# Banded attention per key tile on float32r halves, and split first loads of the full attention, in a two-layer kernel

## The chip, the cores and the metric

One core of one Trainium2 chip. The metric is the device time of one execution of the whole program in microseconds (us), lower is better. Clocks of the profile start at the first instruction of the profiled execution.

## What is computed

Two layers over x of shape (2, 2048, 256), 16 heads of 16 features. Layer 0 is full attention gated by an expert FFN, layer 1 is banded attention gated by a LoRA mixture:

```python
xn = _layernorm(x); s = _L0_attn_ref(xn, ...); g = _silu(_L0_ffn_ref(xn, ...)); x = x + s * g
xn = _layernorm(x); s = _L1_attn_ref(xn, ...); g = _silu(_L1_ffn_ref(xn, ...)); x = x + s * g

# inside _L1_attn_ref: a key counts for a query if it is at most 64 positions away
band = jnp.abs(idx[:, None] - idx[None, :]) <= WINDOW // 2          # WINDOW = 128
scores = jnp.einsum('bhqd,bhkd->bhqk', q, k) * SCALE + jnp.where(band, 0.0, -jnp.inf)
attn = jax.nn.softmax(scores, axis=-1)
out = jnp.einsum('bhqk,bhkd->bhqd', attn, v)
```

## The kernel before

The program is a chain of stages with a barrier of all engines between them: `phase_weights`, `phase_project` (layer 0), `phase_router`, `phase_attend_full`, `phase_combine_experts`, `phase_project` (layer 1), `phase_attend_band`, `phase_combine_lora`. In a stage each engine runs a program of its own, written out by hand, and semaphores tie them. SP issues the loads and stores, and a DMA is issued when the engine's program comes to it, in that order.

Projection (`phase_project`). Eight chunks of 512 tokens. TensorE makes q and k (four blocks of 128 features, `m`) and v; each block of q and k is split into summands that together hold the fp32 value. In layer 0 these are two float32r halves: ScalarE writes the first (L625), VectorE the rest (L543), and SP stores both to `s_halves`. In layer 1 they are three bf16 parts: ScalarE the first (L625), VectorE the remainder `rest` (L548), ScalarE the second part (L630), POOL the third (L472), and SP stores 128 x 3 x 512 bf16 per block to `s_parts` (L420). Per chunk SP also stores xT (four of 128 x 512 fp32, L401) and v (four, L427) and loads x.

Full attention (`phase_attend_full`). Eight groups of four heads, four iterations of 512 queries each. Two heads stand at rows 0 and two at row 64 (`side`), with three sets of 16 rows (high x high, high x low, low x high) and, for the scores, two rows more in which K is 1 and Q holds the two halves of minus the maximum. Before the scores of an iteration can be made, all its maxima must be known: TensorE makes score tiles for maxima (L1074), VectorE reduces them (L965, 32 units an iteration), TensorE turns the maxima, VectorE splits them, and POOL stores them into the rows of Q (`store_maxima`, L923). TensorE then makes the scores (L1100), ScalarE the exponentials (L1027), TensorE the product with V (L1112). At the start SP issues 30 loads of K and Q for group 0 (`load_halves`: per set of rows one of K, 16 x 2 x 2048, and four of Q, 16 x 2 x 512), then four of V; TensorE waits for all 30 and for the rows of ones. TensorE's program writes out iterations 0 to 7 and 24 to 31 and runs 8 to 23 in a loop of two rounds.

Banded attention (`phase_attend_band`). Again eight groups of four heads, in 32 chunks of 512 queries. K and Q hold six sets of 16 bf16 rows (`PART_ROWS`), a padding row with its two sides filled with -1e30, and two rows for the maximum, 99 in all; K is padded by 128 columns at both ends. For each of the 16 query tiles of a chunk TensorE makes a tile for maxima (97 x 128 by 256 keys, L1403), VectorE adds the mask and reduces (L1324), two chunks ahead of the scores. The maxima of a chunk are turned, split, and stored by POOL (`store_maxima`, L1275, two DMAs). Scores are made per chunk and key tile (`TILES`, six a chunk with widths 64, 192, 256, 256, 192, 64, so that tiles at a chunk's edge are made for both chunks), L1434, with the mask added by a product of the identity with the mask in bf16 (L1439). ScalarE takes the exponentials of four heads at once (L1367), TensorE multiplies with V (L1454). Outputs are turned (L1420), divided by VectorE (L1340) and stored by POOL (L1280). K and Q have two buffers; V has one, reloaded by quarters:

```python
with sp.Fori(1, NG - 1) as g:
    values(g)                      # waits for pv_done of the group before, quarter by quarter
    wait_apart(sp, kq_loaded, GROUP_LOADS * DMA * (g + 1), passed)
    load_group(sp, K, Q, S, kq_loaded, g + 1, (g + 1) % 2, TP, P)
```

TensorE waits for `kq_loaded` of a group when the maxima of its first chunk are due (two chunks before its scores), and the groups run in a loop on every engine, with addresses computed in registers.

## Time and profile before

| | us |
|---|---|
| median of 3 runs (2842.24, 2850.95, 2851.11) | 2850.95 |
| the profiled execution, its own time | 2839.8 |
| its span in the profile | 2838.1 |
| stage of full attention: first DMA issue to last output of VectorE | 276.4 to 1731.9 |
| second projection: first VectorE instruction to first DMA issue of the next stage | 2129.1 to 2255.6 |
| stage of banded attention: first DMA issue to last output of VectorE | 2255.6 to 2725.8 |

Shares of the span by engine (busy): TensorE 83%, VectorE 65%, ScalarE 53%, POOL 14%. They are averages over stages with different limits, so what a change of one stage is worth has to be read from that stage: which engine or transfer ends its waits. In the rows below PE is TensorE's matmul, PEld its load of weights, DVE VectorE, ACT ScalarE, SPq the DMA issues of SP. A text in brackets is the idle time before an instruction and what ended it. "PEclk" is the granted TensorE clock as a share of full speed.

### The profile page before, as it was taken

The page shows a single profiled execution, that of the slowest core. Times are in us where ns is not written, and L with a number is a line of the kernel's source. Part 1 is how long each engine was busy: PE and PEld are TensorE (multiplying, and loading weights), DVE is VectorE, ACT ScalarE, POOL GpSimd, SP SyncE. Part 2 cuts the span into 40 slices and gives each one's busy share as a digit, 9 for nine tenths or more (in the row PEclk, how much of TensorE's full clock was granted, in tenths as well). Part 3 has the DMA queues.
Part 4 walks back from the last instruction along what each step waited for, and adds up shares of the span by engine and source line. Part 5 has one row for each costly group of instructions (what it writes and reads, how often), then busy time and mean ns, then how long its engine had stood idle before and what let it go on. Part 6 is the DMA issues. An engine that isn't in the chain of part 4 may idle for free. (4 is left out here: it accounts for less than half of the span.)

```text
span 2838.1 us, 51653 instructions
## 1 busy us (share of the span) xinstructions
PE 2369.1 (83%) x16300; PEld 1335.0 (47%) x16300; DVE 1856.6 (65%) x3220; ACT 1490.0 (53%) x2180; POOL 389.7 (14%) x526
## 2 busy tenths in 40 slices
PE   4786499999999999999999985999986557767788
PEld 2554133333333333333333332888875424534568
DVE  2554689999999989999999950333326445545546
ACT  2343077777777777777777773222223313323333
POOL 0000000000000000000000000333333301111125
PEclk9798599999999999999999997999998869988999
DMA  3777700401304022040400003232407975775555
GB/s 108 237 266 220 95 3 5 64 3 26 41 9 61 3 41 28 10 57 5 58 9 16 6 5 108 60 93 84 118 16 245 252 93 76 98 91 71 82 145 162
DMA packets 209153, 225.10 MB, mean 79 GB/s; under 512 B 59008, under 2 KB 153088, under 8 KB 207488
## 3 DMA queue, kind: packets, MB, share of 16 engines
q1 hardware_dynamic: 196320, 212.70, 35.0%
q0 software_dynamic: 9408, 9.72, 1.7%
q10 hardware_dynamic: 3296, 0.81, 0.3%
q8 instruction: 100, 1.64, 0.3%
q14 instruction: 29, 0.24, 0.0%
HBM read 129.28 MB, written 92.80 MB: 78 GB/s over the span
## 5 line engine op out<-in xcount | busy, mean ns | idle before, releaser
L965 DVE TENSOR_REDUCE a_maxes<-a_ps_a 128x2 f32<-128x1024 f32 x1024 | 1202.5, 1221 | 146.6 <-PE a_ps_a L1074 141.7
L1027 ACT ACTIVATE a_prob<-a_ps_s 128x512 f32<-128x512 f32 (+1 forms) x1376 | 1035.8, 804 | 394.3 <-PE a_ps_s L1100 388.1
L1100 PE MATMUL a_ps_s<-a_Q,a_K 50*128 50x512 f32 x2048 | 593.0, 453 | 91.3 <-ACT a_prob L1027 89.0
L1074 PE MATMUL a_ps_a<-a_K,a_Q 48*128 48x512 f32 x2048 | 551.7, 454 | 55.9 <-DMA a_Q<-s_halves 40.6
L1112 PE MATMUL a_ps_o<-a_prob,a_V 128*32 128x512 f32 x4096 | 547.3, 606 | 0.0
L1100 PEld LDWEIGHTS a_ps_s<-a_Q,a_K 50*128 50x128 f32 x2048 | 278.8, 185 | 505.3 <-ACT a_prob L1027 467.6
L1074 PEld LDWEIGHTS a_ps_a<-a_K,a_Q 48*128 48x128 f32 x2048 | 246.2, 190 | 256.5 <-issue 142.3
L1367 ACT ACTIVATE a_prob<-a_ps_s 128x256 f32<-128x256 f32 (+2 forms) x192 | 142.0, 739 | 299.4 <-PE a_ps_s L1439 299.3
L1324 DVE CUSTOM_DVE_ANT_0 a_masked<-a_ps_a,k_mask 128x256 f32<-128x256 f32 x512 | 186.7, 421 | 110.6 <-PE a_ps_a L1403 110.3
L923 POOL DMA_DIRECT2D a_Q<-a_m_parts x128 | 64.3, 503 | 1309.8 <-DVE a_m_parts L957 1302.9
L1434 PE MATMUL a_ps_s<-a_Q,a_K 99*128 (+3 forms) x768 | 124.9, 247 | 89.2 <-DMA a_Q<-s_parts 73.8
L1112 PEld LDWEIGHTS a_ps_o<-a_prob,a_V 128*32 128x32 f32 x4096 | 81.0, 108 | 149.4 <-issue 98.6
L1403 PE MATMUL a_ps_a<-a_K,a_Q 97*128 (+1 forms) x512 | 98.8, 292 | 54.6 <-DMA a_Q<-s_parts 43.6
L1771 DVE TENSOR_TENSOR c_prod<-c_ps_cy,c_xv 128x1024 f32<-128x1024 f32 x32 | 39.2, 1225 | 160.5 <-issue 103.4
L1434 PEld LDWEIGHTS a_ps_s<-a_Q,a_K 99*128 (+1 forms) x768 | 60.8, 99 | 145.6 <-issue 126.0
L79 PE MATMUL c_ps_xv<-k_AQ,c_xT 128*128 128x512 f32 x384 | 100.2, 411 | 24.3 <-DMA c_att<-s_att 24.3
L1439 PE MATMUL a_ps_s<-k_mask_bf,k_ident_bf 128*128 128x64 bf16 (+2 forms) x768 | 119.9, 245 | 0.0
L79 PE MATMUL p_ps_qk<-p_xT,k_qkv 128*128 128x512 f32 x384 | 103.0, 424 | 16.7 <-DVE p_xT L523 13.0
L1738 ACT ACTIVATE c_eg<-c_ps_out 128x256 f32<-128x256 f32 x32 | 12.3, 384 | 190.2 <-PE c_ps_out L1698 190.2
L79 PE MATMUL c_ps_out<-k_UO,c_pT 128*128 128x256 f32 x768 | 95.8, 281 | 0.0
L1454 PE MATMUL a_ps_o<-a_prob,a_V 128*32 128x192 f32 (+2 forms) x1536 | 94.6, 327 | 0.3 <-ACT a_oT L1373 0.3
L79 PE MATMUL c_ps_cy<-k_BK,c_cT 128*128 128x512 f32 x384 | 94.8, 395 | 0.0
(192 smaller groups left out, 2415.6 us busy)
## 6 DMA issues: line engine op xcount, KB each, us to landing
s_xT<-p_xT SPq DMA_DIRECT2D x64, 256.0 KB, 3.5
s_halves<-p_parts SPq DMA_DIRECT2D x32, 512.0 KB, 4.9
s_v<-p_v_out SPq DMA_DIRECT2D x64, 256.0 KB, 3.5
a_V<-s_v SPq DMA_DIRECT2D x64, 256.0 KB, 3.3
c_xT<-s_xT SPq DMA_DIRECT2D x64, 256.0 KB, 5.0
a_K<-s_halves SPq DMA_DIRECT2D x48, 256.0 KB, 9.2
a_Q<-s_halves SPq DMA_DIRECT2D x192, 64.0 KB, 9.6
s_parts<-p_parts SPq DMA_DIRECT2D x32, 384.0 KB, 3.1
```

The lines of the kernel that those rows point to most:

```text
L79: last = nc.tensor.matmul(out, stationary(s, k), moving(m, k), start=start and n == 0, stop=stop and n == len(passes) - 1, skip_group_chec ...
L965: nc.vector.tensor_reduce(maxes[:, :, slot, qt, kc], ps_a[:, o:o + 2 * CH].rearrange("p (z k) -> p z k", z=2), AX.X, ALU.max).then_inc(a_d ...
L1027: nc.scalar.activation(prob[:, ring:ring + len(t), :].rearrange("p r q -> p (r q)"), ps_s[:, bank:bank + len(t) * CH], ACT.Exp, scale=scal ...
L1074: last = nc.tensor.matmul(ps_a[:, o + side * CH:o + (side + 1) * CH], Q[rows, q0:q0 + P], K[rows, k0:k0 + CH], start=True, stop=True)
L1100: last = nc.tensor.matmul(ps_s[:, bank + x * CH:bank + (x + 1) * CH], K[rows, k0:k0 + P], Q[rows, q0:q0 + CH], start=True, stop=True)
L1112: last = nc.tensor.matmul(ps_o[h * VW:(h + 1) * VW, :], V[:, kt, h * VW:(h + 1) * VW], prob[:, ring, :], start=(kt == 0), stop=(kt == KT - 1),
L1324: nc.vector.tensor_tensor_reduce(masked[:, k % 4, :], ps_a[:, (k % 4) * WIN:(k % 4 + 1) * WIN], W["mask"][:], 1.0, 3 * NEG, ALU.add, ALU.m ...
L1367: nc.scalar.activation(prob[:, j % PROBS, :, 0:hi - lo], s[:, :, 0:hi - lo], ACT.Exp, scale=scale).then_inc(exp_done, 1)
L1403: last = nc.tensor.matmul(ps_a[:, slot * WIN:(slot + 1) * WIN], Q[0:ROW_M, ds(q0, P)], K[0:ROW_M, ds(k0, WIN)], start=True, stop=True, ski ...
L1434: nc.tensor.matmul(ps_s[:, base + r * WIN:base + r * WIN + w], K[:, ds(half * GK + h * TP + P + qc * CH + kt * P, P)], Q[:, ds(half * GQ + ...
L1439: last = nc.tensor.matmul(ps_s[:, base + r * WIN:base + r * WIN + w], W["ident_bf"][:], W["mask_bf"][:, first:first + w], start=False, sto ...
L1454: last = nc.tensor.matmul(ps_o[h * VW:(h + 1) * VW, lo:hi], V[:, 1 + qc * TT + kt, h * VW:(h + 1) * VW], prob[:, j % PROBS, h, 0:hi - lo], ...
```

## The change

1. `phase_router` is gone as a stage. Its instructions (`router_weights_vector`, `router_weights_scalar`) run at the start of `phase_attend_full`.
2. First loads of the full attention: K of group 0 comes per slot (12 loads of 16 x 2048) and Q of the first 512 queries on ScalarE's queue, each with a semaphore of its own; TensorE starts with what it needs. TensorE's loop over iterations 8 to 23 is written out.
3. The projection of layer 1 makes the same float32r halves as that of layer 0. The third part, and POOL's work on it, are gone.
4. `phase_attend_band` is rewritten. K and Q as in the full attention (50 rows at 0 and at 64), no padding, three buffers of K and Q, two of V. The scores go per step of one key tile (128 steps), each key tile once with its window of up to 256 queries; the product with V is cut where a window crosses a chunk. The maxima are made 28 units (14 steps) ahead, two query tiles a unit, and are turned and stored per half group of 1024 queries: eight DMAs of 8 x 128, by SP. The mask is still added by a bf16 product. Outputs are stored by SP. No engine has a loop or register addresses there; POOL has no program in this stage.
5. The weights of layer 0 are freed before layer 1.

The core of the diff:

```diff
@@ phase_project (both layers now)
-                wait_apart(sp, part3, 2 + 4 * c + m + 1, passed)
-                sp.dma_start(S["parts"][m // 2, u, :, (m % 2) * P:(m % 2 + 1) * P, tok].rearrange("a p t -> p a t"),
-                             parts[:, m]).then_inc(parts_stored[m], DMA)
+                wait_apart(sp, rest_ready, NQ + 4 * c + m + 1, passed)
+                sp.dma_start(S["halves"][m // 2, u, :, (m % 2) * P:(m % 2 + 1) * P, tok]
+                             .rearrange("a p t -> p a t"), f32(parts[:, m])).then_inc(parts_stored[m], DMA)
@@ phase_attend_full, sync
-            load_halves(sp, K, Q, S, kq_loaded, 0, 0)
+            for slot in range(PAIR):
+                load_first_keys(sp, K, S, slot, k_first[slot])
+            for qc in range(1, NCH):
+                load_first_queries(sp, Q, S, qc, kq_loaded)
@@ phase_attend_full, scalar
+            load_first_queries(act, Q, S, 0, q_first)
@@ phase_attend_full, tensor
-            pe.wait_ge(rows_set, 4 * DMA)
-            pe.wait_ge(kq_loaded, HALVES_LOADS * DMA)
+            pe.wait_ge(q_first, FIRST_LOADS * DMA)
             for k in range(NU):
+                if k % (NU // PAIR) == 0:
+                    pe.wait_ge(k_first[k // (NU // PAIR)], FIRST_LOADS * DMA)
                 pe.wait_ge(a_done, k + 1)
                 maximum_scores(0, 0, k, bank_of(0, k))
+            pe.wait_ge(kq_loaded, HALVES_LOADS * DMA)
+            pe.wait_ge(rows_set, 4 * DMA)
@@ phase_attend_band, sync (new)
+            load_rows(sp, 1, K, 0, 0, EARLY_K, kq_early)
+            load_rows(sp, 1, K, 0, EARLY_K, T, kq_loaded[0])
+            load_rows(sp, 0, Q, 0, EARLY_Q, T, kq_loaded[0])
+            load_v(sp, 0)
+            store_maxima(0)
+            load_group(1)
+            load_v(sp, 1)
+            for g in range(NG):
+                if g + 2 < NG:
+                    if g > 0:
+                        wait_apart(sp, s_ready, 2 * KT * g, passed)
+                    load_group(g + 2)
+                store_maxima(2 * g + 1)
+                if g > 0:
+                    store_output(NCH * g - 2)
+                    store_output(NCH * g - 1)
+                    if g + 1 < NG:
+                        wait_apart(sp, pv_done, KT * g, passed)
+                        load_v(sp, g + 1)
+                if g + 1 < NG:
+                    store_maxima(2 * g + 2)
+                store_output(NCH * g)
+                store_output(NCH * g + 1)
@@ phase_attend_band, tensor (new)
+            def scores(s, side):
+                if kt == 0 and side == 0:
+                    pe.wait_ge(m_loaded, M_LOADS * DMA * (2 * g + 1))
+                if kt == HALF_QT - 1 and side == 0:
+                    pe.wait_ge(m_loaded, M_LOADS * DMA * (2 * g + 2))
+...
+            for s in range(STEPS + LAG + 2):
+                for side in range(2):
+                    if s < STEPS:
+                        scores(s, side)
+                    unit(2 * s + AHEAD + side)
+                if 0 <= s - LAG < STEPS:
+                    add_values(s - LAG)
```

`unit(a)` makes the two maxima tiles of unit a (`maximum_scores`; for the first unit of a group it first waits for that group's `kq_loaded`) and, one unit after a half group's last, turns the maxima of that half.

How the change moves instructions. On SP, at the start of the full attention, before (names: a_K, a_Q, a_V the tiles in SBUF, s_halves, s_v the tensors in DRAM):

```order
L798 DMA a_K<-s_halves 16x2x2048
L802 DMA a_Q<-s_halves 16x2x512 x4
L798 DMA a_K<-s_halves 16x2x2048
L802 DMA a_Q<-s_halves 16x2x512 x4
L798 DMA a_K<-s_halves 16x2x2048
```

and now:

```order
L751 DMA a_K<-s_halves 16x2048 x12
L760 DMA a_Q<-s_halves 16x2x512 x18
L853 DMA a_V<-s_v 128x512 x4
L728 DMA a_K<-s_halves 16x2x2048
L732 DMA a_Q<-s_halves 16x2x512 x4
```

All K comes first, one slot after the other; six loads of Q have gone to ScalarE's queue, ahead of its rows of ones.

On SP in the banded attention, for groups 1 and 2 of the loop over g (a_m_parts holds the split maxima, s_att the outputs):

```order
L1273 DMA a_K<-s_halves 16x2x2048 x6
L1273 DMA a_Q<-s_halves 16x2x2048 x6
L1293 DMA a_Q<-a_m_parts 1x8x128 x8
L1298 DMA s_att<-a_o_out 128x4x64 x2
L1276 DMA a_V<-s_v 128x2048
L1293 DMA a_Q<-a_m_parts 1x8x128 x8
L1298 DMA s_att<-a_o_out 128x4x64 x2
L1273 DMA a_K<-s_halves 16x2x2048 x6
```

where before POOL, in its loop over chunks, had

```order
L1275 DMA a_Q<-a_m_parts 1x16x128
L1275 ISA
L1275 DMA a_Q<-a_m_parts 1x16x128
L1280 ISA
L1280 DMA s_att<-a_o_out 128x4x64
```

The stores of the maxima and of the outputs have moved from POOL's queue to SP's, and the first store of a group stands behind twelve loads.

On TensorE in the banded attention, one step and the beginning of the next (a_ps_s scores, a_ps_a tiles for maxima, a_ps_o outputs):

```order
L1481 MATMUL a_ps_s<-a_Q,a_K 128x256
L1485 MATMUL a_ps_s<-k_mask_bf,k_ident_bf 128x256
L1481 MATMUL a_ps_s<-a_Q,a_K 128x256
L1485 MATMUL a_ps_s<-k_mask_bf,k_ident_bf 128x256
L1449 MATMUL a_ps_a<-a_K,a_Q 128x256 x2
L1481 MATMUL a_ps_s<-a_Q,a_K 128x256
L1485 MATMUL a_ps_s<-k_mask_bf,k_ident_bf 128x256
L1481 MATMUL a_ps_s<-a_Q,a_K 128x256
L1485 MATMUL a_ps_s<-k_mask_bf,k_ident_bf 128x256
L1449 MATMUL a_ps_a<-a_K,a_Q 128x256 x2
L1500 MATMUL a_ps_o<-a_prob,a_V 32x256 x4
```

Four score products, four of the mask, four for maxima and four with V make a step; a V product of 256 columns takes the place of before's pieces of 64, 192 and 256.

## Rows read from the trace of the kernel before

**Rows 1.** The page, part 1: busy time and share of each engine.
```profile
PE 2369.1 (83%) x16300; PEld 1335.0 (47%) x16300; DVE 1856.6 (65%) x3220; ACT 1490.0 (53%) x2180; POOL 389.7 (14%) x526
```

**Rows 2.** Timeline, start of the first attention: start, length, engine, line.
```profile
271.04 0.69 DVE L1537 TENSOR_REDUCE r_top<-k_logits 128x64 f32<-128x512 f32 x1 [3.07 <-PEq L96]
276.36 0.36 SPq L798 DMA_DIRECT2D a_K<-s_halves  x1
290.94 1.85 SPq L890 DMA_DIRECT2D a_V<-s_v  x4
308.22 1.22 PE L1074 MATMUL a_ps_a<-a_K,a_Q 48*128 48x512 f32 x4 [40.57 <-DMA a_Q<-s_halves]
309.05 11.40 DVE L965 TENSOR_REDUCE a_maxes<-a_ps_a 128x2 f32<-128x1024 f32 x10 [33.36 <-PE a_ps_a L1074]
348.79 2.06 POOL L923 DMA_DIRECT2D a_Q<-a_m_parts  x4 [70.83 <-DVE a_m_parts L957]
355.27 0.63 PE L1100 MATMUL a_ps_s<-a_Q,a_K 50*128 50x512 f32 x2
```

**Rows 3.** Windows; at the end TensorE's clock, DMA share, GB/s.
```profile
216.00:226.00 10.00, 8.59 (x43) 5.56 (x41) 6.16 (x12) 3.80 (x6) 0.00 (x0) 1.00 1.04 375
276.00:308.00 32.00, 0.00 (x0) 0.00 (x0) 0.00 (x0) 0.63 (x1) 1.27 (x2) 0.50 1.02 115
2156.00:2225.00 69.00, 50.35 (x287) 41.98 (x288) 48.59 (x110) 29.55 (x50) 28.72 (x25) 1.00 0.99 309
2356.00:2386.00 30.00, 18.59 (x208) 11.57 (x206) 14.24 (x74) 9.48 (x13) 3.58 (x6) 0.87 1.09 131
```

**Rows 4.** DMA issues, 268 to 310 and 2350 to 2395; last is us to landing.
```profile
a_V<-s_v SPq DMA_DIRECT2D x4, 256.0 KB, 18.2
...
a_Q<-a_m_parts POOLq DMA_DIRECT2D x6, 4.0 KB, 7.0
```

**Rows 5.** Line 973 in windows 340:700 and 690:1110: first and last start.
```profile
L973 DVE TENSOR_REDUCE a_neg_max<-a_maxes x9: 219/219/221, 345.4 to 687.8; 128x16 f32<-128x64 f32 x9
...
L973 DVE TENSOR_REDUCE a_neg_max<-a_maxes x9: 219/220/221, 730.6 to 1076.8; 128x16 f32<-128x64 f32 x9
```

**Rows 6.** Banded stage: timeline, lines' first and last starts, a wait, all waits from 2420.
```profile
2255.59 0.36 SPq L757 DMA_DIRECT2D a_K<-s_parts  x1
...
L1403 PE MATMUL a_ps_a<-a_K,a_Q x512: 269/273/422, 2289.2 to 2706.3; 97*128 x149, 97*128 97x256 bf16 x22
L1434 PE MATMUL a_ps_s<-a_Q,a_K x768: 189/247/422, 2313.3 to 2722.8; 99*128 x168, 99*128 99x64 bf16 x8, 99*128 99x192 bf16 x8, 99*128 99x256 bf16 x8
L1340 DVE TENSOR_TENSOR a_o_out<-a_ps_m,a_recip x33: 423/425/425, 2323.9 to 2725.8; 128x256 f32<-128x256 f32 x33
...
2388.18 0.32 PE L1434 MATMUL a_ps_s<-a_Q,a_K 99*128 x2 [12.43 <-DMA a_Q<-s_parts]
...
PE a_ps_s L1434 <- DMA a_Q<-s_parts: 61.4, 5, 12.8
```

**Rows 7.** Timeline of TensorE: values in the projection, and half a chunk of the band.
```profile
2219.24 3.05 PE L79 MATMUL p_ps_v<-k_qkv,p_xT 128*128 128x256 f32 x24
...
2704.61 0.53 PE L1454 MATMUL a_ps_o<-a_prob,a_V 128*32 128x192 f32 x8
2705.08 0.34 PE L1434 MATMUL a_ps_s<-a_Q,a_K 99*128 99x192 bf16 x2
2705.75 0.81 PE L1403 MATMUL a_ps_a<-a_K,a_Q 97*128 97x256 bf16 x4
2706.40 0.60 PE L1420 MATMUL a_ps_m<-k_ident,a_oT 128*128 128x128 f32 x4
```

**Rows 8.** Groups of instructions (page and lines): count, busy us, mean ns, idle before.
```profile
L1100 PEld LDWEIGHTS a_ps_s<-a_Q,a_K 50*128 50x128 f32 x2048 | 278.8, 185 | 505.3 <-ACT a_prob L1027 467.6
L1324 DVE CUSTOM_DVE_ANT_0 a_masked<-a_ps_a,k_mask 128x256 f32<-128x256 f32 x512 | 186.7, 421 | 110.6 <-PE a_ps_a L1403 110.3
...
L1373 ACT ACTIVATE a_oT<-a_ps_o 128x512 f32<-128x512 f32 x32 | 19.1, 596 | 3.1 <-PE a_ps_o L1454 3.0
```

More of the change, by code:

```diff
@@ L326, in phase_project @@
         cT = n.sb("cT", [P, 2, 2, DK, CH], F32R) if first else None
[L327 to L328 removed]
+        parts = n.sb("parts", [P, 4, 2, CH], F32R)
         v_out = n.sb("v_out", [P, 2, TT, H, VW])
@@ new lines, in phase_attend_band, with window, unit_of, half_of @@
+    LOADS = 2 * 2 * len(HALVES_ROWS)
+    def window(t):
+        lo, hi = max(0, t * P - REACH), min(T, t * P - REACH + WIN)
+        first = lo - (t * P - REACH)
+        return lo, hi, first, first + hi - lo
+    def unit_of(a):
+        g, rest = a // (KT * PAIR), a % (KT * PAIR)
+        return g, 2 * (rest // 4), (rest // 2) % PAIR, 1 - rest % 2
+    def half_of(a):
+        return a // HALF_UNITS
+    def turn_behind(a):
+        return half_of(a) - 1 if a % HALF_UNITS == 1 and HALF_UNITS < a < UNITS + HALF_UNITS else None
@@ new lines, in phase_attend_band, with pieces @@
+    position = {}
+    for a in range(UNITS + 2):
+        if a < UNITS:
+            position["unit", a] = len(position)
+        if turn_behind(a) is not None:
+            position["turn", turn_behind(a)] = len(position)
+    at_position = {p: what for what, p in position.items()}
+    def pieces(s):
+        lo, hi, first, _ = window(s % KT)
+        out = []
+        for c in range(lo // CH, (hi - 1) // CH + 1):
+            q0, q1 = max(lo, c * CH), min(hi, (c + 1) * CH)
+            touches = [t for t in range(KT) if window(t)[0] < (c + 1) * CH and window(t)[1] > c * CH]
+            out.append((NCH * (s // KT) + c, q0 - c * CH, q1 - c * CH, first + q0 - lo,
+                        s % KT == touches[0], s % KT == touches[-1]))
+        return out
```

663 lines of the change are left out of this document (300 added, 363 removed).

## The prediction

> **What bounds the kernel now.** I read the page first, for the busy shares: TensorE 83%, VectorE 65%, no single bound [rows 1]. So each stage has to be read by itself. Then I read the start of the first attention in the timeline [rows 2]. The router stage begins at 271.04, the first load is issued at 276.36, and TensorE starts at 308.22 after 40.57 us of idle time that a DMA ended. VectorE then takes ten maxima in 11.40 us, 1.14 each. The maxima's store is issued at 348.79 and the first score product starts at 355.27. Third, the windows with their DMA columns [rows 3]: while K and Q are loaded (16 rows at a time) the DMA engines are full (share 1.02 to 1.09) and yet move only 115 to 131 GB/s (131 with loads of V among them). Stores over 128 rows move 375 GB/s at the same share. The projection of the second layer runs at share 0.99 and 309 GB/s, so it is bound by its transfers or nearly. Fourth, landings [rows 4]: the four loads of V, issued at 290.94 on SP's queue behind 30 loads of K and Q, land 18.2 us after issue (median), at 309, one us after K and Q are through. Their 1 MB over 128 rows is a matter of 3 us at 375 GB/s; the rest was waiting. **A transfer on SP's queue waits for what was issued on it before.** The maxima's stores, issued on POOL's queue while K and Q load, land in 7.0 us (median). Fifth, the main loop of the first attention [rows 5]: eight rounds take 342.4 us, and the eight that hold the jump back in TensorE's loop 346.2. Sixth, the banded stage [rows 6]: first load 2255.59, first maxima product 2289.2, first score product 2313.3, last output 2725.8. Five times in the later part, and once before, TensorE waits 12 us for a group's K and Q (61.4 us in the five). The granted clock is 0.87 on average over 2356 to 2386 [rows 3], a window that ends in the first of these waits: TensorE falls from 2.4 to 1.2 GHz in such a wait.
>
> **Part 1, start of the first attention.** The router's steps move into this stage, onto VectorE and ScalarE, which idle there until 309. That takes away one stage and its barrier: the first load goes out at 271.4 instead of 276.4, where the router began (5 us). TensorE no longer waits for all 30 loads and for the ones rows, but for six K loads of slot 0 (0.79 MB) and six Q loads of 64 KB (0.39 MB), the latter on ScalarE's queue. 1.18 MB at 115 GB/s is 10 us; with 2 us of landing, the first product comes at 283 (25 us earlier). Slot 1 is needed 16 maxima (18 us) later and is loaded after another 7 us. ScalarE issues ten DMAs ahead of the router's exponential (5 us and some, POOL needed 0.5 each), and the router took 5 us before: VectorE is free at 282, just in time. Bounds: 5 us of loading if two queues double the rate, 15 if the order mixes. The Trainium skill, "DMA: Bandwidth & Descriptors", section "Issuing engines are not separate DMA queues", says that queues of different engines run on the same 16 DMA engines and only save issue time; by it the first product is at 283, and with a doubled rate it would be at 278. The trace agrees with the rule as far as it goes: SP issued all in 15 us and the transfers took 32 [rows 2, 3]. What is late next: the 32 maxima end at 320, the maxima's store goes out at about 324, and the second group's loads (issued at 303, 27.5 us long) still run until 332. In the kernel before the store went out alone and took 6.5 us to the first score product; beside loads I add 3. **Part 1: -22 us** (-17 to -31). The unrolled loop of TensorE removes the 3.8 us of the round with the jump [rows 5]: **-4**.
>
> **Part 2, projection of the second layer.** Removed per chunk: four copies on ScalarE, four subtractions on POOL, and the chain between them. What covers them are the transfers: a chunk moves 4.19 MB, at 309 GB/s 13.6 us. The change stores 2.10 MB of float32r halves in place of 1.57 MB, so 4.72 MB. Of before's 13.6 us, xT's 1.05 MB take 2.8 at 375 GB/s and the rest, 3.15 MB, 10.8 (291 GB/s). After: 3.15 MB of xT and halves 8.4 us, the remaining 1.57 MB 5.4: 13.8 us. Bounds 12.6 (all at 375) and 15.3 (all at 309). Eight chunks: **+2 us** (-8 to +14). So the faster engines gain nothing here.
>
> **Part 3, the banded stage.** Start: K and Q of the first half group are 1.67 MB, on two queues that write the same rows. At 115 GB/s that is 14.5 us, plus 2: first maxima product at 2272.5, 17 us earlier. 17 units of two maxima at 0.365 each (186.7 us of 512, [rows 8]) end at 2285, when the rest of the group has landed too, and m_low comes at 2288; eight stores take SP 4 us and 2 to land, so the first score product is at 2294.
>
> A step (one key tile, four heads), on TensorE [rows 7]: eight float32r products of 256 columns at 0.127 (24 of the projection's values in 3.05 us) 1.02; four mask products at 0.11 (eight of 192 columns in 0.67, so 0.084 x 256/192) 0.44; P times V 0.5 (for 192 columns 0.47 pass until the next score product, most of it a fixed part); a quarter of the output's transposes 0.15; maxima's transpose and edges 0.09. That is **2.2 us a step**. VectorE: four maxima 1.46, a quarter of the normalising and an eighth of the splits 0.35: 1.8, hidden. ScalarE: two exponentials of 512 at 0.6 (as the copy of 512, [rows 8]) and a quarter of that copy: 1.35, hidden. Before needs 2.65 for as much (413 us from first score product to last output, less 74 of wait, over 128). Bounds: 2.0 (no transposes, no edges) and 2.65 (as before).
>
> Where the waits go. Unit 32, the first of group 1, stands at step 2, in TensorE's order ahead of everything else, and waits for K and Q of group 1. SP issues them after the first maxima's store (2292), and 3.15 MB at 115 GB/s are 27.4: landed at 2322. Then the maxima of half 1 are stored, on SP's queue **behind V and the loads of group 2**: these drain at 2352, the store lands at 2353, and step 7 waits for it. The same comes back in every group that loads one: SP issues the loads of group g+2 when the scores of g-1 are done, that is at the first step of g, and the store of the second half's maxima after them. It was ready at step 3 but lands 30 us after the group's start (27.5 of drain, some 2.5 of issue and landing), and step 7 needs it at 15.4. So a group costs 30 + 1.5 (my allowance for the lower clock after the wait) + 9 x 2.2 = 51.3, where the steps alone are 35.2. Three buffers remove the wait for K and Q and the moved store puts one of the same size in its place. V and the output stores, also on SP now, are small beside that: an output waits for its o_done without holding anything that is due.
>
> Sum: 2353 + 1.5 + 9 x 2.2 = 2374 (end of group 0); groups 1 to 5, 256.5: 2631; groups 6 and 7 load nothing, 70.4: 2701; tail of three steps 6: last output at 2707, against 2726. **-19 us.** With s the step, the end is 2518 + 86 s. Bounds: s from 2.0 to 2.65 gives -36 to +20; six drains at 131 GB/s give another -21, at 105 +15.
>
> **Total**: -22 - 4 + 2 - 19 = -43. The profiled execution took 2839.8 (span 2838.1), so 2797; the median of the three runs is 2850.95, 11 above, and the changed kernel should stand there too: **2808**.
>
> **The rivals.**
> A, the maxima's stores aren't held back. For it: on POOL's queue they landed in 7.0 us beside loads, each is 4 KB, and an order of landing on one queue is seen for V only. Against: these four landings of V, 18.2 us late. Then only the wait at step 2 is left: 2322 + 126 x 2.2 + 6 = 2605, -121; total -145: 2706. The Trainium skill, "DMA: Bandwidth & Descriptors", section "Queues, rings and completion order", says both: each DMA engine takes descriptors in ring order, and completion is not first in, first out for an issuing engine, because a DMA may use fewer than 16 engines. By the first, my sum; by the second, 2706 would need idle engines. The trace agrees with the first. Chance 0.12.
> B, the projection runs at 309 GB/s whatever it stores: 15.3 a chunk, +14 in place of +2: 2820. For it: the share was already 0.99. Against: the first layer's window at 375. Chance 0.05.
> C, slower: float32r weights aren't hidden. In the first attention of the kernel before each load stands beside 512 columns; here one comes every 256. If a load (0.185, [rows 8]) and the product's columns (0.11) follow each other, eight take 2.3 and a step 3.5: end 2819, +93; total +69: 2920. It decides above s = 2.7, where the stage eats the 24 us of parts 1 and 2. Against: 24 products of 256 float32r columns, each with its own load, in 3.05 us [rows 7]. Chance 0.05.
> My forecast, 0.78.
>
> **Numbers.** 2808. My case by itself, with its bounds not all on one side: 2750 to 2845. A, at 2706, stays outside, and C too; to leave out no more than 2 in 10 I take 2740 to 2845. A measurement of this kernel can tell 0.3%, 9 us, from no change: the line is at 2842. Faster: A, B and all of mine but its upper end, 0.90; same 0.04; slower 0.06.
>
> **What would show it.** First maxima product of the first attention near 283 (303, if only the barrier is gained). Chunks of the second projection still 13 to 14 us with DMA share near 1 and POOL idle. In the banded stage: a wait of TensorE of some 20 us at unit 32, then six waits of 14 to 19 us on the DMA of m_parts, DMA share 1 at 110 to 130 GB/s in the first 28 us of each group, and no wait for K and Q after the first. Steps of 2.2 us between. I am wrong if a group of 16 steps takes 36 us (rival A), if the maxima's stores land in under 8 us, if steps take 3, or if the projection falls to 11 us a chunk.

## The result, and the profile after

The changed kernel takes 3113.14 us (median of 4 runs, 3111.44 to 3119.31) against 2848.3 for the kernel before beside it: a ratio of 1.0937, 95% interval 1.0912 to 1.0962. It is 265 us slower, where 2808 was predicted. The profiled execution took 3113.3, its span is 3111.3.

The page of the changed kernel, parts 1 and 2 (busy time; the span in 40 slices, granted TensorE clock in tenths), which answers to [rows 1]:

```profile
PE 2767.2 (89%) x15640; PEld 1508.8 (48%) x15640; DVE 1846.4 (59%) x3167; ACT 1483.1 (48%) x2211; POOL 291.0 (9%) x391
...
PE   4786899999999999999997799997469999999989
...
PEclk9897899999999999999999899998655555555569
```

TensorE is busy for 398 us more than before, with fewer instructions, and in the last quarter of the span the clock stands at half. By stages:

| | before | after | difference |
|---|---|---|---|
| last output of the full attention | 1731.9 | 1705.7 | -26.2 |
| first load of the band | 2255.6 | 2222.75 | -32.8, so -6.6 in between |
| band, first load to last output | 470.2 | 779.1 | +308.9 |
| last output of the band to the end | 112.3 | 109.5 | -2.8 |

These sum to +273 us, the difference of the two spans. The start of the full attention, in the timeline of the changed kernel (start, length; answers to [rows 2]):

```profile
271.68 6.11 SPq L751 DMA_DIRECT2D a_K<-s_halves  x12
271.69 2.78 ACTq L760 DMA_DIRECT2D a_Q<-s_halves  x6
277.83 9.20 SPq L760 DMA_DIRECT2D a_Q<-s_halves  x18
...
283.75 1.22 PE L1045 MATMUL a_ps_a<-a_K,a_Q 48*128 48x512 f32 x4 [15.69 <-DMA a_Q<-s_halves]
```

The first product for maxima comes at 283.75, where 283 was forecast. Second projection, SP's stores of halves in two neighbouring chunks, and the windows of the stage (clock, DMA share, GB/s at the end; answers to [rows 3]):

```profile
2184.94 4.16 SPq L402 DMA_DIRECT2D s_halves<-p_parts  x4
...
2197.17 4.31 SPq L402 DMA_DIRECT2D s_halves<-p_parts  x4
```

```profile
2130.00:2199.00 69.00, 57.88 (x326) 50.58 (x325) 49.54 (x117) 22.25 (x35) 6.01 (x6) 0.93 1.04 358
```

Over seven chunks (first stores issued at 2120.24 and at 2209.05) one takes 12.7 us. The DMA engines are full as forecast, but move 358 GB/s.

The band: all score products and all outputs (duration; first and last start), then one step's worth of TensorE and of its weight loads in the timeline, then the windows.

```profile
L1481 PE MATMUL a_ps_s<-a_Q,a_K x512: 359/579/580, 2262.5 to 2994.8; 50*128 50x256 f32 x149, 50*128 50x192 f32 x22
...
L1369 DVE TENSOR_TENSOR a_o_out<-a_ps_o,a_recip x32: 424/425/425, 2333.2 to 3001.8; 128x256 f32<-128x256 f32 x32
```

```profile
2600.89 0.58 PE L1481 MATMUL a_ps_s<-a_Q,a_K 50*128 50x256 f32 x1
2601.40 0.39 PE L1485 MATMUL a_ps_s<-k_mask_bf,k_ident_bf 128*128 128x256 bf16 x1
2601.73 0.58 PE L1481 MATMUL a_ps_s<-a_Q,a_K 50*128 50x256 f32 x1
2602.24 0.40 PE L1485 MATMUL a_ps_s<-k_mask_bf,k_ident_bf 128*128 128x256 bf16 x1
2602.56 0.79 PE L1449 MATMUL a_ps_a<-a_K,a_Q 48*128 48x256 f32 x2
...
2605.39 1.08 PE L1500 MATMUL a_ps_o<-a_prob,a_V 128*32 128x256 f32 x8
```

```profile
2600.89 0.28 PEld L1481 LDWEIGHTS a_ps_s<-a_Q,a_K 50*128 50x128 f32 x1 [0.60 <-issue]
2601.40 0.10 PEld L1485 LDWEIGHTS a_ps_s<-k_mask_bf,k_ident_bf 128*128 128x128 bf16 x1 [0.22 <-issue]
2601.72 0.28 PEld L1481 LDWEIGHTS a_ps_s<-a_Q,a_K 50*128 50x128 f32 x1 [0.22 <-issue]
```

```profile
2300.00:2400.00 100.00, 94.47 (x396) 49.58 (x395) 29.39 (x146) 22.01 (x38) 0.00 (x0) 0.50 0.49 61
...
2900.00:3000.00 100.00, 100.00 (x455) 47.88 (x455) 14.02 (x63) 26.23 (x45) 0.00 (x0) 0.50 0.04 9
```

A score product starts 0.51 us before the mask product behind it, and that 0.33 us before the next. The weight load of each begins only when the product before it is through: the 0.22 us of idle time ahead of a load is what 256 columns take at 1.2 GHz (0.213), and 0.28 + 0.22 is the 0.51. So load and columns follow each other. The clock is 0.50, 1.2 GHz, in every window read between 2230 and 2990, though TensorE is never idle in the last of them. In the kernel before it came back between the waits; a few microseconds after the wait that ended at 2388.18 [rows 6]:

```profile
2392.00:2394.00 2.00, 1.96 (x25) 1.29 (x27) 1.69 (x9) 1.42 (x3) 0.00 (x0) 1.00 0.07 18
```

The waits of the stage (2236 to 3005):

```profile
PE a_ps_a L1449 <- DMA a_Q<-s_halves: 52.9, 3, 33.0
PE a_ps_s L1481 <- DMA a_Q<-a_m_parts: 6.8, 2, 5.5
```

Some 18 us of the first row are the wait at unit 32; the waits for the maxima's stores, 88 us in my sum (six of 14.6), are hardly there. From first score product to last output 739 us pass; without these two waits 714 remain for 128 steps and the tail, 5.5 us a step, as in the timeline (2600.89 to the end of the values at 2606.4).

### The profile page after: what moved, and what is told of

It reads as the page before. It is cut to its first block and busy times, and to the rows that moved or that the text cites. A ratio compares the mean times of both kernels' runs of the same rounds, so it can differ in the third digit from the quotient of the medians.

```text
span 3111.3 us, 45980 instructions
## 1 busy us (share of the span) xinstructions
PE 2767.2 (89%) x15640; PEld 1508.8 (48%) x15640; DVE 1846.4 (59%) x3167; ACT 1483.1 (48%) x2211; POOL 291.0 (9%) x391
## 5 line engine op out<-in xcount | busy, mean ns | idle before, releaser
L932 DVE TENSOR_REDUCE a_maxes<-a_ps_a 128x2 f32<-128x1024 f32 x1024 | 1202.5, 1221 | 114.3 <-PE a_ps_a L1045 109.5
L996 ACT ACTIVATE a_prob<-a_ps_s 128x512 f32<-128x512 f32 (+1 forms) x1376 | 1035.9, 805 | 368.9 <-PE a_ps_s L1071 362.9
L1071 PEld LDWEIGHTS a_ps_s<-a_Q,a_K 50*128 50x128 f32 x2048 | 278.6, 185 | 506.2 <-ACT a_prob L996 456.2
L1341 DVE CUSTOM_DVE_ANT_0 a_scratch<-a_ps_a,k_mask 128x256 f32<-128x256 f32 (+1 forms) x512 | 191.1, 413 | 471.2 <-PE a_ps_a L1449 471.1
L1399 ACT ACTIVATE a_prob<-a_ps_s 128x512 f32<-128x512 f32 (+1 forms) x256 | 149.5, 584 | 587.8 <-PE a_ps_s L1485 587.8
L1045 PEld LDWEIGHTS a_ps_a<-a_K,a_Q 48*128 48x128 f32 x2048 | 246.0, 189 | 229.8 <-issue 103.5
L1481 PE MATMUL a_ps_s<-a_Q,a_K 50*128 50x256 f32 (+1 forms) x512 | 274.7, 536 | 6.8 <-DMA a_Q<-a_m_parts 6.8
L1449 PE MATMUL a_ps_a<-a_K,a_Q 48*128 48x256 f32 (+1 forms) x512 | 196.9, 492 | 54.1 <-DMA a_Q<-s_halves 52.9
L1481 PEld LDWEIGHTS a_ps_s<-a_Q,a_K 50*128 50x128 f32 x512 | 151.5, 296 | 129.7 <-issue 118.9
L1485 PE MATMUL a_ps_s<-k_mask_bf,k_ident_bf 128*128 128x256 bf16 (+1 forms) x512 | 198.4, 388 | 0.0
L1449 PEld LDWEIGHTS a_ps_a<-a_K,a_Q 48*128 48x128 f32 x512 | 126.7, 309 | 108.1 <-DMA a_Q<-s_halves 53.7
L1874 POOL TENSOR_TENSOR c_sums<-c_sums,c_gate 128x256 f32<-128x256 f32 x64 | 47.4, 741 | 936.3 <-DVE c_gate L1867 936.2
L1500 PE MATMUL a_ps_o<-a_prob,a_V 128*32 128x192 f32 (+2 forms) x1408 | 134.3, 508 | 0.0
L1485 PEld LDWEIGHTS a_ps_s<-k_mask_bf,k_ident_bf 128*128 128x128 bf16 x512 | 53.3, 104 | 111.2 <-issue 111.2
```

Of the source, the lines that this page charges most:

```text
L932: nc.vector.tensor_reduce(maxes[:, :, slot, qt, kc], ps_a[:, o:o + 2 * CH].rearrange("p (z k) -> p z k", z=2), AX.X, ALU.max).then_inc(a_d ...
L996: nc.scalar.activation(prob[:, ring:ring + len(t), :].rearrange("p r q -> p (r q)"), ps_s[:, bank:bank + len(t) * CH], ACT.Exp, scale=scal ...
L1045: last = nc.tensor.matmul(ps_a[:, o + side * CH:o + (side + 1) * CH], Q[rows, q0:q0 + P], K[rows, k0:k0 + CH], start=True, stop=True)
L1071: last = nc.tensor.matmul(ps_s[:, bank + x * CH:bank + (x + 1) * CH], K[rows, k0:k0 + P], Q[rows, q0:q0 + CH], start=True, stop=True)
L1341: nc.vector.tensor_tensor_reduce(scratch[:, (2 * a + x) % (2 * BANKS), first:last], ps_a[:, o + first:o + last], W["mask"][:, first:last], ...
L1399: nc.scalar.activation(prob[:, s % RING, side, :, first:last], scores[:, :, first:last], ACT.Exp, scale=scale).then_inc(exp_done, 1)
```

## The experiments

Three things are to be explained: why load and columns don't overlap, why the clock stays down, and where the forecast waits are. The theories named in the expectations: **D** (drain), products on 64 rows and on 128 rows can't follow each other without emptying the array; **K** (kind), it is float32r and bf16 in turn; **O**, the order; **L**, these products are too light to lift the clock; **C**, the clock stays where the stage was entered. W in one expectation says that the clock has another cause than how much TensorE does.

The diffs are written in short, with words for the kernel's own calls. A run for which no ratio is given was made once, and the runs were made on several chips. The kernel before, measured beside them, took 2843 to 2854 us, so a difference under some 15 us between two such runs is taken for nothing. A turn is the place in TensorE's program where a product of 64 rows or fewer follows one of more, or the other way round; the changed kernel has four of them a side in each step, besides those around the products with V.

### Order of the products, a warm entry, more and fewer mask products

`g1_grouped`: per side both score products, then both mask products. In it the second score product starts a sum in a bank where the first slot's sum is still open, so the first slot's scores are not right; h5, below, starts each bank once and keeps the sums.

```diff
-for slot: score(slot); mask(slot)
+for slot: score(slot)
+for slot: mask(slot)
```

> Per side the two score products come first, then the two mask products, as in the kernel before; the rest is as changed. In the changed kernel the granted clock is 0.50 in every stretch of the band, a step takes 5.5 us, a score product 0.51 us from its start to the next one's and a mask product 0.33. Theory O (order: the change of type at every product keeps weight loads from being hidden, and with them TensorE too thinly used for the clock to rise): two of four such changes go; the step falls well below 5.5 us, or the clock rises to 1.0 and the step to about 2.5 us, total near 2830. Theory L (the light products themselves, float32r on 48 to 50 rows by 256 columns, hold the clock down in whatever order): clock stays 0.50, band within 5% of 740 us, total 3080 to 3120. Theory C (a stage entered at half clock stays there): as L.

Measured 3026.2 us. Two turns fewer between heights per side save 87 us, 0.17 us a turn, at a clock of 0.50. A shorter step, but neither what O gives (2.5 us or well below 5.5) nor L's total (3080 to 3120); L is right on the clock here.

`g2_warm`: products into an unused bank while the first loads are awaited.

```diff
+for _ in range(170):
+    matmul(ps_s[:, 2 * CH:2 * CH + WIN], ident_bf, mask_bf[:, 0:WIN])
 for a in range(AHEAD): unit(a)
```

> 170 extra products (identity by mask, bf16, 128 rows, 256 columns) into an unused bank at the start of the band's TensorE program, which fill the wait for the first loads (about 2216 to 2240), so that the first product for maxima is entered at full clock. Nothing else is changed. Theory C (entered at half clock, stays at half clock; entered at full clock, stays at full): clock 1.0 on from the fill, step about 2.5 us, total near 2830, unless a later wait lets it fall for good. Theories O and L (the stream itself can't hold the clock): 1.0 in the fill and for some microseconds after, then 0.50 again, total 3100 to 3115.

Measured 3121.2. The fill and what follows it, in windows:

```profile
2246.00:2250.00 4.00, 4.00 (x38) 3.35 (x35) 0.00 (x0) 0.00 (x0) 0.00 (x0) 1.00 1.12 151
...
2254.00:2260.00 6.00, 5.95 (x17) 4.36 (x18) 6.00 (x35) 0.00 (x0) 0.00 (x0) 0.51 0.79 197
```

The clock fell back while TensorE made maxima (48 rows, VectorE pacing them), before any step. So `w2_warm_at_scores` put 100 such products directly ahead of the first score product.

> The changed kernel with 100 extra products of 128 rows just ahead of the first score product of the stage, behind the wait for the maxima, so that the steps themselves are entered at full clock (the earlier fill stood ahead of 28 units of maxima, in which the clock fell back to 0.5). At half clock the fill costs up to 20 us. Theory C (a step at half clock keeps itself there, one at full clock would stay at full): step about 2.8 us on from here, total 2780 to 2830. Theory L (these steps can't hold the clock): 1.0 for some microseconds, then 0.50 for the rest of the band, total 3115 to 3135.

Measured 3125.2. Its timeline from the end of the fill on shows steps at both clocks:

```profile
2293.11 0.30 PE L1486 MATMUL a_ps_s<-a_Q,a_K 50*128 50x256 f32 x1
2293.34 0.28 PE L1490 MATMUL a_ps_s<-k_mask_bf,k_ident_bf 128*128 128x256 bf16 x1
2293.55 0.38 PE L1486 MATMUL a_ps_s<-a_Q,a_K 50*128 50x256 f32 x1
...
2294.94 0.58 PE L1486 MATMUL a_ps_s<-a_Q,a_K 50*128 50x256 f32 x1
2295.45 0.40 PE L1490 MATMUL a_ps_s<-k_mask_bf,k_ident_bf 128*128 128x256 bf16 x1
```

Up to 2294.6 a side takes 1.28 us (2293.11 to 2294.39), so a step with its values, transposes and edges (0.5 + 0.15 + 0.09, the prediction's terms) 3.3 us at 2.4 GHz; that is an estimate from one side, as no run shows a whole step of this stream at 2.4 GHz. Without a wait, the next products run at 1.2 GHz, and the windows say 0.50 from then on. C is out: this stream doesn't hold the high clock, and the total is the one that L gave. And 3.3 us at full clock is far above 2.2: two faults, not one.

`g3_mask_twice`: each mask product twice.

```diff
+    mask(slot)
     mask(slot)
```

> Each mask product is made twice (-2e30 in place of -1e30 outside the band, same weights after each other), four products of 128 rows by 256 columns more per step. At half clock these cost 4 x 0.21 = 0.9 us a step or more: 128 x 0.9 = 110 us, total about 3220, if the clock stays at 0.50 (theory W: the clock has another cause than how much TensorE does). Theory L, and in part O: more 128-row columns a microsecond bring the clock to 1.0, the step falls to about 3 us though it does more, total 2860 to 2920, below the changed kernel.

Measured 3209.9, clock 0.50 throughout. The second mask product, same height and behind its like, starts 0.19 us after the first (2501.95, 2502.14), with no gap of the loads between: two products of one height do overlap, though both add to the same sum in PSUM. The total is the one given for a clock that stays (about 3220), and not L's 2860 to 2920: more 128-row columns alone didn't lift the clock.

`g4_no_mask`: no mask products.

> The mask products are left out (weights of keys outside the band are not zeroed), so that the stream is float32r products of 48 to 50 rows alone, apart from the products with V. At half clock: the step loses at least 4 x 0.33 = 1.3 us, to 4.2 us, total about 2945. Theory O (change of type): with all changes of type gone weight loads of float32r hide behind products, clock 1.0, step about 2 us, total 2780 to 2820. Theory L: clock 0.50, as even the 128-row products are gone; score products still 0.4 us apart or more.

Measured 2777.6, 335 us less than the changed kernel for 512 products of 0.11 us at full clock, 0.33 at half. The score products of one side and the products for maxima of the other now start together:

```profile
2499.86 0.38 PE L1481 MATMUL a_ps_s<-a_Q,a_K 50*128 50x256 f32 x1
2499.87 0.38 PE L1449 MATMUL a_ps_a<-a_K,a_Q 48*128 48x256 f32 x1
...
2500.79 0.64 PE L1497 MATMUL a_ps_o<-a_prob,a_V 128*32 128x192 f32 x16
```

The clock is back in part of the stage (0.72 on average from 2400 to 2500, 0.64 to 2600), which L excludes: products of 48 to 50 rows don't hold it down by themselves. O gave 2780 to 2820. And the forecast waits are there, nine of them:

```profile
PE a_ps_s L1481 <- DMA a_Q<-a_m_parts: 100.6, 9, 18.5
```

`h3_no_mask_same_side` asks whether it is the side by side that helps.

```diff
-return g, 2 * (rest // 4), (rest // 2) % PAIR, 1 - rest % 2
+return g, 2 * (rest // 4), (rest // 2) % PAIR, rest % 2
```

> The run without mask products (2777.6 us) with one difference: the products for maxima that stand behind the scores of a side are on the same 64 rows as these, not on the other 64. Same instructions, same sizes. Theory D: neighbours can't run side by side within a unit (only at the turn from one side to the other), the step grows by at least 4 x 0.11 us at full clock, more at half, total 2850 or more. Theory K, and any theory in which only the number of products counts: total within 15 us of 2777.6.

Measured 2783.0, within the 15 us that K allows and far from the 2850 or more that D gave: a miss for D. It decides little on D itself. The trace shows that the change took little of the side by side away, because the products of one side still meet those of the other where the sides turn: eight products take 0.76 us (2504.35 to 2505.11, clock 1.00), less than the 0.85 that their 2048 columns would take one after the other. And the waits for maxima, 92.5 us here, shrink where steps grow.

### Height or kind

`h1_mask_rows`: the same kinds in turn, but the mask made on the side's own 64 rows, by two products for one.

```diff
-mask: ident_bf[128 rows] x mask_bf[128 rows]
+mask: ident_bf[r] x mask_bf[r], then ident_sw_bf[r] x mask_sw_bf[r], r = the side's 64 rows
```

The `_sw` constants hold the other half of the identity and of the mask on these rows.

> The mask product of 128 rows becomes two of 64 rows on the same 64 rows as the score product (for each side constants with the halves of the identity and of the mask are there; same sum, twice the mask columns). In the changed kernel 0.22 us passes without a weight load before every mask product and before every score product behind one; in the run without mask products score products of one side and products for maxima of the other start 10 ns apart. Theory D (drain: products on rows 0 to 63 and on rows 64 to 127 run side by side, and a 128-row product can't begin before both are done, nor they before it): no such gap is left, the step falls below 4 us though it has 4 products more, total 2850 to 2950. Theory K (kind of number: bf16 after float32r costs the gap): the gaps stay, with four products more the step is 6 us or longer, total 3150 or more.

Measured 2851.6 us, 261 us less than the changed kernel, with 512 products more. Its weight loads at 1.2 GHz:

```profile
2499.74 0.33 PEld L1504 LDWEIGHTS a_ps_s<-a_Q,a_K 50*128 50x128 f32 x1
2500.16 0.14 PEld L1510 LDWEIGHTS a_ps_s<-k_mask_bf,k_ident_bf 64*128 64x128 bf16 x1
2500.19 0.14 PEld L1510 LDWEIGHTS a_ps_s<-a_mask_sw_bf,a_ident_sw_bf 64*128 64x128 bf16 x1
```

None of these loads has a gap ahead of it. In the whole stage the changed kernel has 111.2 us of idle time ahead of its 512 mask loads, and h1 19.0 us ahead of its 1024. At 1.2 GHz a step takes about 3.8 us (42 score products, four a step, in the 40 us from 2640), in place of 5.5; part of that is products of the two sides running side by side. `k1_full_height` is the other way round: score products over 114 rows, the mask as it was. Its scores hold the sums over both sides.

```diff
-rows = slice(side * SIDE, side * SIDE + ROW_M0 + 2)
+rows = slice(0, SIDE + ROW_M0 + 2)
```

> The changed kernel with score products over rows 0 to 113, both sides' rows at once, in place of 50 rows (the rows between are zeroed at the start, which delays the stage by some 10 us; the scores then hold both heads' sums, so their weights are not the reference's). Products for maxima stay at 48 rows. Same number, types, order and columns of products. Theory D (turn between 64 and 128 rows keeps the weight load from being hidden): no gap before mask products and between the score products of a slot and the next, gaps only around the products for maxima; the step at the same clock 1 us or more shorter at 2.4 GHz (at 1.2 GHz 5.5 to 4.3 or less), total 2960 or less, and far less if the clock rises with it. Theory K (float32r and bf16 in turn): the 0.22 us gaps stay before every mask product, total 3110 to 3130.

Measured 2929.4 us. Timeline, at 1.2 GHz as above:

```profile
2501.53 0.58 PE L1490 MATMUL a_ps_s<-a_Q,a_K 114*128 114x256 f32 x1
2501.92 0.44 PE L1494 MATMUL a_ps_s<-k_mask_bf,k_ident_bf 128*128 128x256 bf16 x1
2502.01 0.56 PE L1490 MATMUL a_ps_s<-a_Q,a_K 114*128 114x256 f32 x1
2502.37 0.44 PE L1494 MATMUL a_ps_s<-k_mask_bf,k_ident_bf 128*128 128x256 bf16 x1
2502.74 0.79 PE L1458 MATMUL a_ps_a<-a_K,a_Q 48*128 48x256 f32 x2
```

```profile
2501.91 0.15 PEld L1494 LDWEIGHTS a_ps_s<-k_mask_bf,k_ident_bf 128*128 128x128 bf16 x1
2501.92 0.35 PEld L1490 LDWEIGHTS a_ps_s<-a_Q,a_K 114*128 114x128 f32 x1
...
2502.74 0.50 PEld L1458 LDWEIGHTS a_ps_a<-a_K,a_Q 48*128 48x128 f32 x2 [0.22 <-issue]
```

Two scores and their masks take 1.21 us (2501.53 to 2502.74) in place of 1.67 (2600.89 to 2602.56), and here the only gap is ahead of the 48-row products. float32r and bf16 still alternate: K is refuted from both sides, D stands. That the mask adds to the sum its score product has just begun isn't the reason either, as here and in g3 the loads overlap all the same. The whole step came out longer than D gave: about 5 us at 1.2 GHz (64 mask products, four a step, in the 80 us from 2470) and not 4.3 or less, because the maxima, at 48 rows, now stand between two turns of their own (0.72 us in place of 0.60). The Trainium skill, "TensorEngine Tiling (Array Packing)", section "Key Properties", says that changing the tiling mode, not merely the tile, drains TensorE. The traces agree, and give the price here: at every turn the load (at 1.2 GHz 0.10 us for the mask, 0.28 for scores) comes behind the columns instead of beside them.

`h5_one_mask`: one 128-row mask product of 512 columns per side, in place of two of 256.

> One mask product of 128 rows by 512 columns per side in place of two by 256, behind both score products. Same columns, two instead of four turns to 128 rows and back per step, two weight loads fewer. Theory D: at half clock 2 x 2 x 0.22 = 0.9 us less a step: 128 x 0.9 = 115 us, total near 3000; grouping alone, with two mask products behind each other, gave 3026. If the clock rises on the way, much less, 2830 to 2900.

Measured 3025.5: 88 us less than the changed kernel, where D gave 115, and the same as g1. What the two share is the number of turns, two per side instead of four.

The clock in k1 tells one thing more. The same steps run at either level for tens of microseconds:

```profile
2450.00:2460.00 10.00, 7.24 (x62) 4.53 (x62) 4.67 (x24) 3.12 (x6) 0.00 (x0) 0.94 1.02 123
2460.00:2470.00 10.00, 4.35 (x24) 3.00 (x28) 1.01 (x5) 1.19 (x2) 0.00 (x0) 0.50 0.69 156
2470.00:2480.00 10.00, 10.00 (x47) 6.14 (x39) 3.56 (x18) 2.98 (x5) 0.00 (x0) 0.50 0.00 1
...
2550.00:2560.00 10.00, 10.00 (x61) 6.02 (x53) 4.29 (x21) 2.98 (x5) 0.00 (x0) 0.61 0.00 0
2560.00:2570.00 10.00, 10.00 (x88) 6.71 (x87) 6.27 (x31) 4.56 (x8) 0.00 (x0) 1.00 0.02 5
```

It falls in a wait, stays at half for 80 us of work without idle time, and comes back. In the changed kernel, which enters the stage at half clock after a wait, it doesn't come back, and in w2 it fell again without a wait.

### Where the waits for maxima come from, and a faster version

`h4_row_groups`: mask as in h1 but 512 columns at once, the program alternating between the two sets of 64 rows, and the maxima's stores on POOL's queue.

```diff
+S0 M0 S1 M1 | maskA S'0 | maskB S'1 | maskA' M'0 | maskB' M'1
-sp.dma_start(Q[row ...], m_parts ...)
+pool.dma_start(Q[row ...], m_parts ...)
```

> No 128-row product but the transposes and the products with V: mask by products of 64 rows on the side's own rows (512 columns each, both slots at once, two per side), program order alternating between the two sets of rows (score, maximum, score, maximum, then mask of side 0 beside scores of side 1, mask of side 1 beside maxima). The stores of the maxima go to POOL's queue (idle in this stage), so they don't stand behind loads. Theory D with the clock following the load: clock near 1.0, per step each half of the rows has 2048 columns = 0.85 us, with values 0.5 and transposes 0.15 1.5 us; VectorE's 1.8 us a step becomes the bound: band 256 to 300 us, total 2640 to 2700. If the clock stays at 0.50 in spite of it: 3 us a step, total about 2800. Theory K: above 3000.

Measured 2742.5 us, below both kernels but above the 2640 to 2700 expected. The steps are short enough (TensorE busy 24 to 31 of 40 us) that TensorE waits again, up to 19 us each:

```profile
PE a_ps_s L1501 <- DMA a_Q<-a_m_parts: 117.0, 8, 19.0
```

A group takes 47.9 us (loads issued at 2328.79, 2376.64, 2424.49). The stores are on a queue of their own and yet take 15 us to land (median). That median mixes two kinds. The eight issued from 2383.77 on, behind the twelve loads of a group (2376.64 to 2382.11), and the eight issued from 2417.17 on, with no such loads ahead:

```profile
a_Q<-a_m_parts POOLq DMA_DIRECT2D x8, 4.0 KB, 18.2
...
a_Q<-a_m_parts POOLq DMA_DIRECT2D x8, 4.0 KB, 1.6
```

The kernel before shows the same: of its six stores between 2350 and 2395 [rows 4] the two behind the first loads of a group took 7.0 us, the two behind most of them 12.9, and the two behind none 1.6. `h6_row_groups_sp` puts the stores back on SP's queue.

> The row-group version (2742.5 us) with the stores of the maxima on SP's queue as in the changed kernel, and not on POOL's. In the row-group version they are on POOL's queue and yet take 15 us to land (7.0 in the kernel before) and TensorE waits 98 us for them in 7 pieces. Theory Q (my prediction's: what holds a store back is its place behind the loads on SP's queue): more waiting than on POOL, total at least 10 us above 2742.5. Theory E (the loads fill the 16 DMA engines, and a store waits there whatever queue it came from): within 10 us of 2742.5.

Measured 2747.2 us, within the 10 us. So small a difference between two single runs says nothing by itself, but TensorE doesn't wait longer either: 100.3 us in 9 pieces, against 117.0 in 8. No effect of the queue is seen, as E says. `h7_stores_first` holds the loads back until the maxima are ready and issues them in two pieces:

```diff
-wait(s_ready, 2 * KT * g); load_group(g + 2)
+wait(m_low, 2 * g + 2); load K of g + 2; ...; wait(m_low, 2 * g + 3); load Q of g + 2
```

> The row-group version (2742.5 us) with SP's order changed: the K half of a group's loads is issued only behind the store of the second half's maxima, the Q half behind the store of the next group's first maxima; outputs between. The loads of a group take some 27 us of the DMA engines, a group then takes as long as its 16 steps (1.8 us, 29 us) or these loads. Theory E: the waits of 15 to 19 us on maxima go, group period from 48 to 31 to 36 us, seven groups: 85 to 120 us less, total 2625 to 2665. If the waits have another cause (latency of the stores themselves): above 2720.

Measured 2751.5 us (ratio to before 0.9685, 0.9664 to 0.9705): no gain on h4, where 2625 to 2665 was expected: a miss. The two queues are released by the same semaphore, and SP is faster:

```profile
2362.98 3.98 POOL L1343 DMA_DIRECT2D a_Q<-a_m_parts  x8 [18.87 <-DVE a_m_parts L1376]
```

```profile
2362.78 3.58 SPq L1278 DMA_DIRECT2D a_Q<-s_halves  x6
```

The loads went out beside the stores, and 14 waits of 8 us took the place of 8 longer ones. `h8_stores_ahead` puts the stores on SP's queue, ahead of each piece:

```diff
+store_maxima(2 * g + 1); load K of g + 2; load_v(g + 1); ...
+store_maxima(2 * g + 2); load Q of g + 2
```

> Row groups as in the 2742.5 us version, loads in two pieces as in the 2751.5 us one, but the stores of the maxima on SP's queue, each set of eight just ahead of the piece of loads (in the 2751.5 us version POOL issued its eight over 4 us, in which SP had issued six loads, and TensorE still waited 111 us in 14 pieces of 8 us). Theory E (a store waits behind the loads issued before it, whatever queue): the waits for maxima shrink to under 3 us each, a group takes 31 to 36 us in place of 48, total 2630 to 2670. If they have another cause: above 2720.

Measured 2715.6 us (ratio 0.9552, 0.9518 to 0.9587): 4.5% faster than the kernel before and 27 us faster than h4, but not the 2630 to 2670 expected. The row for K and Q includes the 30.1 us before the first product of the stage:

```profile
PE a_ps_a L1474 <- DMA a_Q<-s_halves: 77.1, 8, 30.1
...
PE a_ps_s L1509 <- DMA a_Q<-a_m_parts: 15.8, 6, 5.3
```

The waits for maxima are down to 15.8 us, as E says; the Q half, issued later, is now late in its turn. A group takes 42 us (2381.53 to 2423.86), of which the loads fill some 27.

### Part 1 alone

`p1_first_attention`: the kernel before with the changes in the full attention and the router only.

> The kernel before with part 1 alone (first loads of the full attention on two queues and in pieces, router inside that stage, TensorE's loop written out); projection and band as before. The two traces give 24.5 us for the start and 2 to 3 for the loop: total 2820 to 2825. If part of it is given back later (a load delayed elsewhere), 2830 or more.

Measured 2818.4 us (ratio 0.991, 0.9892 to 0.9929): 25 us gained, a little more than expected, none of it given back.

## Why the prediction was wrong

**Part 1** was right in its mechanism and its sum: -22 and -4 forecast, -26.2 in the profile, and -25 when made alone. That the sum came out to 0.2 us is luck. VectorE has the first iteration's maxima at 321.0 in place of 345.4, 24.4 us earlier, and the rest of the stage takes only 1.8 us less: two small errors that cancel. The first product came 0.75 us off. That queues of two engines gained issue time and no rate agrees with the landing at 283.7.

**Part 2** was mis-sized by 8.6 us. I had +2, from 13.8 us a chunk; it is 12.7 us and -6.6, near my lower bound, because the whole stage moved 358 GB/s and not 375 for some of its bytes and 291 for the rest. That the engines freed there gain nothing by themselves agrees with the full DMA share.

**Part 3** failed at one term: the step of 2.2 us. The start was right (first product for maxima 17.4 us after the first load, 16.9 forecast; first score 22.3 later, 21.5 forecast), and so was the wait at unit 32. The step rested on two rows: 24 float32r products in 3.05 us, each with its load hidden, and mask products at 0.11 us [rows 7]. Both are streams of one height (128 rows, and 99 beside 128), and I put them together as if a stream of 50, 128 and 48 rows in turn would run like them. I looked at the kind of number, at columns and at loads, and never at the change of height, which the change brings into the band four times a side. In the runs it makes the step 3.3 us at 2.4 GHz, 1.1 above my term; "if steps take 3" was one of my signs of being wrong. My rival C had the mechanism nearly (load and columns one after the other, 3.5 us, 2920), with the cause wrong, float32r as such, and at 0.05.

The second fault is the clock, and it is the larger one. The prediction has it only as 1.5 us after each wait, in the expectation that a busy TensorE gets it back as in the kernel before. Here it doesn't, and 3.3 us become 5.5. Either fault was enough to leave my range: by my own formula, end 2518 + 86 s, a step of 3.3 us gives 2802 in place of 2707, and a total of about 2903. The rest, some 210 us, is the clock.

The sum by these: from first score product to last output I had 413 us, which is 282 for steps and 131 for waits and tail. Steps at 3.3 us add 141, the half clock adds 282, and about 100 us of waits go, since in 88 us per group the loads are through long before the stores are wanted: 736, and 739 were measured. The agreement is no proof of the split, as the 5.5 us and the waits that are left were read from the same trace; the split between 3.3 and 5.5 rests on w2.

**The waits** were therefore forecast for a kernel that didn't come about. Where the steps are short (g4, h4, h6), they are there: 100 to 117 us in eight or nine pieces of up to 19, and 48 us a group where I had 51.3. Only my reason, "behind V and the loads on SP's queue", was too narrow, since POOL's queue gave the same: the stores land behind the loads that were issued before them (18.2 us, against 1.6 without loads ahead). The Trainium skill, "DMA: Bandwidth & Descriptors", section "Issuing engines are not separate DMA queues", says that DMAs of different engines run on the same 16 DMA engines and interleave. The traces agree with the first; of a store that gets in between the loads they show nothing, and there the measurement decides. Rival A is thereby refuted. The 7.0 us on which it rested was the middle one of 1.6, 7.0 and 12.9.

**What stays open**: what it is in a stream of products that brings the clock back. Shown is that the changed kernel, g1, g2, g3, h5 and w2 have it at 0.50 in all their steps, but for the 5 us behind w2's fill; that in w2 it fell without a wait; and that in g4, h3, h1, k1, h4, h6, h7 and h8 it is high in part of the stage. None of the theories O, L and C gives all of this. The number of turns alone doesn't sort them: k1 has two per side, as g1 and h5 have, and gets the clock back where these don't; it differs from them in the rows of its score products (114 against 50). No run varies the rows, the columns per microsecond and the turns one at a time at a fixed clock, so the cause is not settled.

## What to carry to other kernels

Before products of different height (64-row and 128-row) are put next to each other, count the turns and price each with a whole weight load behind the columns (0.17 us a turn at 1.2 GHz in g1); a product that makes the same sum at the neighbour's height can be cheaper even if it takes twice as many columns (h1: 512 products more, 261 us less). A TensorE that is 100% busy is no sign of full speed: read the granted clock beside it, and price a step at both levels. A small store that others wait for belongs ahead of bulk loads in time of issue; another queue doesn't get it past them.

## What was not expected of the hardware

- 740 us of TensorE with hardly any idle time at 1.2 GHz, on one core; and in k1 the same steps for 80 us at 1.2 and then at 2.4 GHz.
- A mask product of 0.11 us at full clock (128 rows) cost 335 us / 512 = 0.65 us each in the changed kernel. That includes the clock, which came back in part without them; the waits that came back, 94 us, would make it more.
- Products on rows 0 to 49 and on rows 64 to 111 start 10 ns apart and run side by side: eight of 256 columns in 0.76 us at full clock (h3).
